# Two-layer graph attention on one core: the spread of the maximum moves into the middle of a stage's first tile, and in the second layer's stages the exponentials and the transposes move earlier

## The reference

```python
h = jnp.maximum(_layernorm(x, axis=-1), 0.0)
x = x + _L0_gnn_ref(h, adj, L0_gnn_W, L0_gnn_a)
h = jnp.maximum(_layernorm(x, axis=-1), 0.0)
x = x + _L1_gnn_ref(h, adj, L1_gnn_W, L1_gnn_a)
# inside a layer (layer 0; layer 1 is the same with -1e9 and without elu):
Wh = jnp.einsum('bni,io->bno', h, W)
e = (Wh @ a1)[:, :, None] + (Wh @ a2)[:, None, :]
e = jnp.where(e > 0, e, ALPHA * e)
attention = jax.nn.softmax(jnp.where(adj > 0, e, neg), axis=2)
return jax.nn.elu(jnp.einsum('bnm,bmo->bno', attention, Wh))
```

## Time and profile before

| what | value |
|---|---|
| median of 3 runs | 293.67 us (293.5 to 296.63) |
| the profiled execution, its span | 293.36 us, 291.6 us |
| PE busy | 285.7 us (98%), granted clock 1.000 of full speed |
| DVE busy | 256.6 us (88%) |
| ACT busy | 191.6 us (66%) |
| DMA | 85.31 MB, mean 293 GB/s |
| q1, the queue of SyncE | 84.50 MB, 77.2% of the engines' span |
| PE L996, the sums | 227.8 us |
| DVE L720, the masks | 155.2 us in 125 of them |

### The profile page before, as it was taken

The page is one execution under the profiler, slowest core; times in us unless marked ns, Lnnn a source line. Parts: engine busy times, 40 slices in busy tenths (PEclk is TensorE's granted clock), DMA queues, the critical chain, the costliest instruction groups (busy, mean ns, idle before and its releaser), DMA issues.

```text
span 291.6 us, 6615 instructions
## 1 busy us (share of the span) xinstructions
PE 285.7 (98%) x2527; PEld 284.2 (97%) x2527; DVE 256.6 (88%) x524; ACT 191.6 (66%) x496; POOL 81.5 (28%) x159
## 2 busy tenths in 40 slices
PE   7999999999999999999999999999999999999896
PEld 7999999999999999999999999999999999999796
DVE  4798899898999989899998989799797979498986
ACT  3386876795878779495886959476575748552500
POOL 2712804306060340705124070603307050000000
PEclk9999999999999999999999999999999999999999
DMA  7999949599495968869494985969859598696912
GB/s 243 414 407 407 367 103 415 210 313 412 166 415 224 371 248 336 331 197 414 145 395 192 328 338 195 372 245 360 314 208 371 204 363 334 250 373 218 347 79 74
DMA packets 25387, 85.31 MB, mean 293 GB/s; under 512 B 3966, under 2 KB 5132, under 8 KB 25356
## 3 DMA queue, kind: packets, MB, share of 16 engines
q1 hardware_dynamic: 24780, 84.50, 77.2%
q10 hardware_dynamic: 576, 0.39, 0.4%
HBM read 80.62 MB, written 4.26 MB: 291 GB/s over the span
## 4 chain that ended last, share of the span: by engine, by line
PE 82%; DMA 8%; ACT 4%; DVE 3%; issue 1%; POOL 0%; SPq 0%; DVEq 0%; POOLq 0%
PE acc L996 62%; PE prj L924 8%; PE tp L861 4%; DMA row_mem<-sqr 4%; DMA in_row<-row_mem 4%; ACT row_r L467 2%; PE acc L1011 2%; PE acc L853 2%; ACT accs L482 2%; DVE pbuf L720 1%; DVE accs L746 1%; PE prj L896 1%; PE prj L1011 1%; PE prj L996 1%; PE acc L905 1%
## 5 line engine op out<-in xcount | busy, mean ns | idle before, releaser
L996 PE MATMUL acc<-wh,pbuf 128*128 128x129 f32 x1968 | 227.8, 275 | 1.6 <-DVE accs L746 1.3
L996 PEld LDWEIGHTS acc<-wh,pbuf 128*128 128x128 f32 x1968 | 223.9, 192 | 2.1 <-issue 1.8
L720 DVE SCALAR_TENSOR_TENSOR pbuf<-row_r,sqr,adj_sb 128x1024 f32<-128x1024 f32 x125 | 155.2, 1278 | 7.2 <-ACT row_r L467 7.2
L482 ACT ACTIVATE accs<-accs,rec 128x128 f32<-128x128 f32 x120 | 36.7, 389 | 41.5 <-DVE rec L756 41.5
L310 POOL TENSOR_TENSOR mean<-stats 128x8 f32<-128x8 f32 x14 | 13.5, 968 | 139.6 <-DVE stats L608 138.4
L414 ACT ACTIVATE xn<-x_sb,shift,rstd 128x128 f32<-128x128 f32 x120 | 47.7, 479 | 0.0
L467 ACT ACTIVATE row_r<-in_row 128x1024 f32<-128x1024 f32 x14 | 29.5, 2106 | 15.5 <-DMA in_row<-row_mem 15.5
L439 ACT ACTIVATE wh<-prj,wh 128x128 f32<-128x128 f32 x120 | 32.9, 366 | 0.0
L924 PE MATMUL prj<-w_ext,hT 128*128 128x130 f32 x240 | 29.3, 275 | 0.0
L339 POOL TENSOR_TENSOR rstd<-vareps,neg_half 128x8 f32<-128x8 f32 x15 | 26.9, 1794 | 6.9 <-DVE vareps L627 5.8
L924 PEld LDWEIGHTS prj<-w_ext,hT 128*128 128x128 f32 x240 | 28.0, 191 | 0.0
(11 more groups left out here) (109 smaller groups left out, 169.8 us busy)
## 6 DMA issues: line engine op xcount, KB each, us to landing
adj_sb<-in_adj SPq DMA_DIRECT2D x64, 1024.0 KB, 10.7
in_row<-row_mem SPq DMA_DIRECT2D x13, 641.0 KB, 4.1
x_sb<-in_x SPq DMA_DIRECT2D x7, 512.0 KB, 10.1
out_x<-x_sb SPq DMA_DIRECT2D x7, 512.0 KB, 12.0
in_row<-row_mem SPq DMA_DIRECT2D x1, 512.0 KB, 4.6
x_sb<-in_x ACTq DMA_DIRECT2D x1, 256.0 KB, 3.5
x_sb<-in_x SPq DMA_DIRECT2D x1, 256.0 KB, 3.3
row_mem<-sqr SPq DMA_DIRECT2D x14, 4.0 KB
```

What stands on the lines that cost most here:

```text
L482: op = nc.scalar.activation(hp[:, t, :], hp[:, t, :], ACT.Copy, scale=rec[:, t:t + 1])
L720: nc.vector.scalar_tensor_tensor(pbuf[:, t, :], row_r[:, n % 2, :], sqr[:, n % 2, 0, t:t + 1], adj_at(n, t), ALU.max, ALU.min).then_inc(p_ ...
L996: mm = nc.tensor.matmul(sum_at(k, s), pbuf[:, t, i * P:(i + 1) * P], wh[:, n % 2, t, :], start=(t == 0 and s == 0 and k < NB), stop=(t == ...
```

## The change

Four edits, each a move; no instruction is added or removed.

1. PE: `spread_emax(n + 1)` moves from behind tile 0 to ahead of matmul 4 of tile 0, in all stages 1 to 14.
2. ACT, n = 9 to 14: `copy_u(n)` and `exps(n + 1)` stand ahead of `scale_accs(n - 1)`. For n = 1 to 8 the order stays.
3. DVE, n = 9 to 14: `exp_args(n + 1)` stands ahead of mask 2 instead of behind it.
4. PE, n = 9 to 13: `transposes(n + 2)` stands behind tile 4 (the fifth) instead of behind tile 5.

```diff
@@ block.scalar @@
                 if n == LAST:
                     seed_last()
-                scale_accs(n - 1)
-                if n < LAST:
+                if n < LAST and not elu:
                     if n % 2 == 0:
                         copy_u(n)
                     exps(n + 1)
+                scale_accs(n - 1)
+                if n < LAST:
                     if elu:
+                        if n % 2 == 0:
+                            copy_u(n)
+                        exps(n + 1)
                         elu_exp(n - 1)
@@ block.vector @@
                 copy_e(n + 1)
-                masks(n, (DRAIN,))
-                exp_args(n + 1)
+                if l == 0:
+                    masks(n, (DRAIN,))
+                    exp_args(n + 1)
+                else:
+
+                    exp_args(n + 1)
+                    masks(n, (DRAIN,))
                 masks(n, range(DRAIN + 1, 6))
@@ block.tensor @@
-            def attend(n, tiles):
+            def attend(n, tiles, emax_of=None):
+
...
+                        if t == 0 and i == T // 2 and emax_of is not None:
+                            spread_emax(emax_of)
...
-                attend(n, (0,))
-                spread_emax(n + 1)
-                attend(n, (1, 2, 3, 4, 5))
+
+                k = 6 if stages[n - 1][0] == 0 else 5
+                attend(n, (0,), emax_of=n + 1)
+                attend(n, range(1, k))
                 if n + 2 <= LAST:
                     transposes(n + 2)
-                attend(n, (6, 7))
+                attend(n, range(k, T))
```

## The result

The changed kernel takes 292.07 us in the median of 19 runs (291.79 to 293.51), the kernel before 293.67 in 19 (292.05 to 297.17). The ratio is 0.9949, with a 95% interval of 0.9928 to 0.9970: 0.9 to 2.1 us faster. The profiled execution took 292.01 us, its span is 290.1 us, 1.5 less than before.

A forecast was written before the change was run, and what follows sets the result against it. TensorE's own work bounds the steady part, plus its 1.34 us wait for the late row at stage 15. The row 0.89 us earlier cuts that wait to 0.45: 293.67 - 0.9 = 292.8 us, range 292.2 to 294.2.

The forecast's parts named there:

- What bounds the kernel: Stages 11 and 14: TensorE's own instructions; only its 1.34 us wait at the head of stage 15 can be won.
- The lead of the write: Iterations 9 to 14: the row leaves 0.89 us earlier, with L430 of stage 11 at 208.79.
- I take the intervals as they are and shift them: Row reads from stage 9 on: all 0.89 us earlier at unchanged intervals, the last at 265.26.
- The limit of 1.34 us: Head of stage 15: TensorE's wait of 1.34 us is all that any of the four moves can win.
- The wait as TensorE's to lose on L746: Head of stage 15: TensorE waits 1.34 us for L746 to empty acc; 0.45 us should be left.
- The sum: Whole kernel: last row 0.89 us earlier, TensorE resumes at 273.35 instead of 274.24, so -0.9 us.
- The spread in mid tile: Tile 0: emax ready 0.15 us before TensorE needs it in odd stages, some 0.22 us more in even ones.
- Mask 2: VectorE, behind `exp_args`: ends at 209.94, 0.27 us before TensorE wants it at tile 2.
- It goes nowhere: Iterations 1 to 8: at most 0.27 us of VectorE idle time won, without use since TensorE has no wait there.
- Rival B: Row reads: they don't move, the write only waiting longer behind adj in ring order; 293.7 us, chance 0.2.
- C: Tile 0 spread: emax comes late to TensorE; 295.4 us at 0.3 us past the cover; chance 0.14, 0.04 past 1%.
- D: Stages with moved transposes: they wait for the normalisation past 0.9 us cover; 0.2 us in each of 5 gives 293.8; chance 0.04.

The follow-up runs named there:

- iteration 11 alone: Kernel before with edits one to three in iteration 11 only, all other iterations in the old order: 292.54 us, ratio 0.9964.
- the early spread: Changed kernel with the spread three matmuls earlier still, ahead of matmul 1 of tile 0: 297.52 us, ratio 1.0139.
- the other queue: Kernel before with the row's two writes to HBM issued by ScalarE on its own queue instead of by SyncE: 293.38 us, ratio 1.000.
- the kernel with late stores: Kernel before with the stores of graphs 0 to 6 issued behind the last adj load: 291.85 us, ratio 0.9951.
- the kernel with all iterations changed but 11: Kernel before with edits one to three in all iterations but 11, which keeps the old order: 291.98 us, ratio 0.9953.

## Why the prediction was right or wrong

- **What bounds the kernel** was right: PE's own work to the head of stage 15, and there the row. Nothing was won before 259 us. The start even came 0.1 us later (stage 11's tile 0 at 206.75 against 206.65).
- **The lead of the write** was right: L430 of stage 11 at 208.89, forecast 208.79, with that 0.1 us in it:

```profile
208.89 0.22 ACT L430 ACTIVATE sqr<-args 128x24 f32<-128x24 f32 x1 [6.10 <-DVE args L691]
```

- **"I take the intervals as they are and shift them"** is the step that failed. 0.89 us was forecast for the last read, 2.13 measured. An interval has two parts which the sum had as one: the batch's last packet, and what the write still waits for behind it. In stage 11 the second part fell from 1.27 to 0.60 us, because the write got past a 16 KB instruction fetch. The write's own lead, which I had put at nothing in stages 11 to 14, is what does it in iteration 11 alone: 0.65 us with no lead of the batch. Of the first part's 1.51 us, 0.68 are the shift that I had forecast; the other 0.83 lie within the scatter of that part between traces, and whether the change caused them stays open. The prediction had called the intervals the weak point; the range took no account of it.
- **The limit of 1.34 us** was too low. The idle time of a view counts from the modelled end of the last record, which reaches some 0.16 us beyond the start of the next in an unbroken stream (records overlap). With the second and third edit alone a shown wait of 0.39 cost 0.55, in the early spread one of 0.30 cost 0.47. By this 1.34 is worth 1.50, which is what the spans differ by. The prediction's lower end, 292.3 for "the full 1.34", and with it 292.2, was made from the shorter number. With 1.50 the same working gives 292.17 and 292.07, the time that was measured.
- **The wait as TensorE's to lose on L746**: right for the old order, but incomplete. Behind it stood VectorE's list to mask 7, without slack: had I asked for the next deadline I would have seen that mask 7, done at 279.74 + 3.67 = 283.41, is due there at 281.47 + 9 x 0.223 = 283.48, behind the nine matmuls of tiles 4 to 6 that the last stage does first. It didn't change the sum, since the row moves both.
- **The sum** of 0.9 us stands against 1.5 in the profiled spans and 1.6 in the medians. With the row 2.13 us earlier, VectorE free at 268.7 takes over as the limit (I had put it at 268.8), and 268.72 - 270.31 gives 1.59. Two errors partly hid each other here: the row's lead was forecast at less than half, and about a quarter of what it turned out to be couldn't be used.
- **The spread in mid tile**: cover enough, as forecast; cmax waits for the spread at 207.96 with emax ready at 207.39. **Mask 2** likewise, and the second and third edit alone show what it costs without the cover. **The normalisation** ended at 214.86 for transposes at 215.80: 0.9 us as worked out. **The transposes'** place: nothing.
- **"It goes nowhere"**, said of the 0.27 us in iterations 1 to 8, holds for those stages. But the first edit alone won nearly everything; its 0.3 to 0.6 us on the writes were enough.
- **Rival B** fell: the reads moved more than the writes. The ring order on which it leant doesn't decide, as the other queue shows. The slowest engine's end of the batch does and, in stage 11, the instruction fetch. Rivals **C** and **D** have no wait in the profile after.

## What to carry to other kernels

Where TensorE is busy for 98%, find the one place where it isn't, and follow it back to the resource with a period of its own; here transfers that slip against the stages. A small write is done when the last of the 16 engines has done its share, so look at its last packets and at what stands in front of them, instructions too: some tenths of a us at the issue can be worth more than themselves. Before removing a wait in front of an engine, ask for the next deadline of the list that feeds it: the wait may only move. Several small moves are not a sum: one of these was worth all of the gain, one cost 2.4 us without its partner, and one was worth nothing.

## What was not expected of the hardware

- A 4 KB write is answered in 1.42 us when the DMA engines are idle (stage 9 of before), and in up to 4.62 us behind a batch of 5.1 MB, by the last nine of its 144 packets; its own queue doesn't change that (3.08 to 4.17 us).
- With almost idle engines it still took 3.17 us in stage 11 of the kernel with late stores, behind one 16 KB instruction fetch of 1.20 us. In the kernel with all iterations changed but 11 the fetch started behind the write's last packet, and the answer took 1.75 us. No run moved the fetch on purpose. In stage 12 of four of the kernels with earlier writes, the changed one not among them, the read again comes 1.62 to 1.79 us behind the batch's last packet, right behind the end of such a fetch, so that it can hold the row there too.
- A release from VectorE to a waiting transpose took 0.06 us in stage 11 of the kernel with the spread ahead of matmul 1, from the end of emax to the start of the matmul (211.38 to 211.44).
